# One program order for five engines and the DMA queue, written anew: x loads, context loads, stores and transposes in another sequence, and one scratch tile moved

## The chip, the cores and the metric

One core of a Trainium2 chip runs the whole program. The time is the device time of one execution in microseconds (us); the median of three runs is compared.

## What is computed

The reference is a gated layer over 2 x 1024 rows of width 2048, in float32:

```python
q1 = fake_quant(layernorm(x), x1_scale, x1_zp)      # 8-bit steps, kept as integers
q2 = fake_quant(ctx, x2_scale, x2_zp)               # (2, 2048, 2048)
x  = x + tanh(g_xattn[0]) * (q1 @ q2)
n  = layernorm(x)
logits = n @ route_w.T                              # 8 experts, the best one is taken
h  = n @ A[e].T                                     # rank 16 for each of the 8 experts
x  = x + tanh(g_ffn[0]) * (route_weight * h) @ Bw   # only the chosen expert counts
```

## The kernel before, in words

**Tiles.** The 2048 rows are 16 tiles t of 128 rows, tiles 0 to 7 of batch 0 and 8 to 15 of batch 1. For each tile TensorE computes four units (t, nb), 512 columns each, of 16 matmuls; `main(t, nb, run)` is a quarter of one, four matmuls. The context of a batch is quantised once into `q2`: 16 pieces of 1 MB per batch (`load_ctx(n)`, pieces 0 to 15 and 16 to 31). ScalarE quantises a piece from its landing place (`stage`, and early on `yT` and `y`) to int8 (`affine_ctx`), GpSimd or ScalarE casts it to bf16 (`widen_ctx`). A piece of batch 1 is cast when the main units of tile 7 for its column block are done.

**The way of a tile.** `load_x(t)`; VectorE's statistics (`stats1`); GpSimd's scale (`first_norm`); ScalarE to int8 (`affine_x`); GpSimd to bf16 (`widen_x`) in the single buffer q1. Then q1 is transposed: by TensorE for tiles 0 to 5 (`turn_q1`, read back by VectorE in `take_q1T`), by a DMA transpose for the others (`flip_q1`). Then the main units; VectorE adds each to x and takes statistics (`add_main`, `stats2_sum`); GpSimd's scale (`second_norm`); ScalarE writes the normed rows as a float16 high part and in full (`norm_high`, `norm_full`), GpSimd subtracts for the low part (`low_rows`). Both parts are transposed by DMA (`flip_high`, `flip_low`) for tiles 2 to 14, and by TensorE (`turn_y`) for 0, 1 and 15. TensorE multiplies them with the router and A (`h_rows_high`, `h_rows_low`, `h_group`), VectorE picks the expert (`gate`, about ten small instructions), TensorE turns the scaled result (`turn_wh`), ScalarE reads it (`take_wh`), TensorE makes four `expert_product(t, g)` of three matmuls each in two PSUM banks `outp`, VectorE adds each to x (`add_experts`), which frees the bank. `store(t)` writes the rows out.

**One tile is finished in another way.** `OUT_ACT = [14]`: for tile 14 ScalarE scales the product into a scratch tile (`scale_part`, line 835) and GpSimd adds it (`add_part`, line 612). The scratch tile lies in `yn`, the source of the flips.

**Places.** x tiles share eight homes (`HOME`, eight places for 16 tiles): `load_x(t)` waits until the tile that had the home before has been stored. x(8) takes the home of tile 3, x(9) that of tile 4, x(10) that of tile 5. `load_ctx(n)` from piece 18 on waits for `affine_ctx(n - 2)`.

**Order.** Nothing is scheduled by the machine: for each engine the calls stand in a list, one list for SP, GpSimd, ScalarE, VectorE and TensorE, and every call waits for its semaphores when its turn comes. All big transfers are issued from SP's list, lines 374 (x), 383 (ctx), 402 (stores), 413, 418 and 422 (flips). A call that waits holds up all that stand behind it on its engine. Engines are joined only by the semaphores.

## Time and profile before

| | us |
|---|---|
| median of 3 runs | 371.43 |
| lowest, highest | 370.81, 371.92 |
| the profiled execution | 371.31 |
| its span (first to last instruction) | 369.5 |
| TensorE busy (matmuls) | 335.8 |
| VectorE, ScalarE, GpSimd busy | 263.2, 193.9, 175.9 |

The span is the time of the profiled execution less 1.8 us around it. Busy time says how much an engine works, not whether it is waited for. In the timeline of an engine a bracket after a row gives the idle time before it and who ended that; the chain of waits follows the last instruction back to what released it, step by step. A DMA has two times: how long its issue held SP, and how long it took from issue to landing, which the chain shows.

### The profile page before, as it was taken

The page shows a single profiled execution, that of the slowest core. Times are in us where ns is not written, and L with a number is a line of the kernel's source. Part 1 is how long each engine was busy: PE and PEld are TensorE (multiplying, and loading weights), DVE is VectorE, ACT ScalarE, POOL GpSimd, SP SyncE. Part 2 cuts the span into 40 slices and gives each one's busy share as a digit, 9 for nine tenths or more (in the row PEclk, how much of TensorE's full clock was granted, in tenths as well). Part 3 has the DMA queues.
Part 4 walks back from the last instruction along what each step waited for, and adds up shares of the span by engine and source line. Part 5 has one row for each costly group of instructions (what it writes and reads, how often), then busy time and mean ns, then how long its engine had stood idle before and what let it go on. Part 6 is the DMA issues. An engine that isn't in the chain of part 4 may idle for free.

```text
span 369.5 us, 5800 instructions
## 1 busy us (share of the span) xinstructions
PE 335.8 (91%) x2214; PEld 183.7 (50%) x2214; DVE 263.2 (71%) x552; ACT 193.9 (52%) x124; POOL 175.9 (48%) x224
## 2 busy tenths in 40 slices
PE   0259999999999989999999889999999999999883
PEld 0124455555766644645464545564465546555361
DVE  3858895798968787783858769748748483774874
ACT  1698299766967480388996453424062424040060
POOL 2396575703334552385977238345257343423041
PEclk9999999999999999999999999999999999999999
DMA  7999998686679999999999799978659361974226
GB/s 313 390 353 395 396 347 307 244 306 260 231 243 227 198 368 194 356 255 289 163 331 259 196 355 157 291 132 269 114 229 172 129 129 30 184 235 96 114 116 227
DMA packets 98066, 88.68 MB, mean 240 GB/s; under 512 B 76004, under 2 KB 77028, under 8 KB 93924
## 3 DMA queue, kind: packets, MB, share of 16 engines
q1 hardware_dynamic: 98016, 88.15, 81.9%
q8 instruction: 26, 0.43, 0.5%
q14 instruction: 12, 0.10, 0.1%
q10 hardware_dynamic: 12, 0.00, 0.0%
HBM read 52.49 MB, written 16.78 MB: 187 GB/s over the span
## 4 chain that ended last, share of the span: by engine, by line
PE 64%; DMA 14%; DVE 9%; ACT 5%; SPq 3%; issue 3%; POOL 2%; ACTq 0%; DVEq 0%; POOLq 0%
PE main L1552 39%; PE outp L1552 5%; DMA xs<-in_x 4%; DVE bn L966 3%; PE hp L1580 3%; DMA qa<-q 3%; PE hp L1576 3%; PE hp L1577 3%; DMA stage<-in_ctx 3%; PE outp L1621 2%; PE outp L1623 2%; PE outp L1622 2%; ACT c L730 2%; ACT x L748 2%; DMA yT<-yn 2%
## 5 line engine op out<-in xcount | busy, mean ns | idle before, releaser
L1552 PE MATMUL main<-q,qa 128*128 128x512 bf16 x880 | 202.9, 384 | 4.5 <-DMA qa<-q 2.8
L1552 PEld LDWEIGHTS main<-q,qa 128*128 128x128 bf16 x880 | 85.5, 99 | 104.7 <-issue 5.3
L585 POOL TENSOR_TENSOR yn<-y,yn 128x2048 f16<-128x2048 f32 x13 | 53.0, 4079 | 31.8 <-ACT y L783 31.7
L1099 DVE SCALAR_TENSOR_TENSOR xs<-main,cc,xs 128x512 f32<-128x512 f32 x46 | 34.2, 743 | 32.2 <-PE main L1552 32.1
L730 ACT ACTIVATE c<-stage,zpc,inv 128x2048 int8<-128x2048 f32 x24 | 49.8, 2086 | 7.9 <-DMA stage<-in_ctx 7.9
L592 POOL CAST q<-c 128x2048 bf16<-128x2048 int8 x24 | 45.8, 1929 | 12.7 <-ACT c L730 10.1
L570 POOL TENSOR_SCALAR ve<-mv 128x1 f32<-128x1 f32 x16 | 3.5, 220 | 84.3 <-DVE mv L1106 84.3
L966 DVE BATCH_NORM_STATS2 bn<-xs 128x6 f32<-128x512 f32 x52 | 32.1, 680 | 14.4 <-DMA xs<-in_x 14.4
L777 ACT ACTIVATE yn<-xs,sc 128x2048 f16<-128x2048 f32 x11 | 23.0, 2093 | 35.6 <-POOL sc L579 35.6
L1153 DVE SCALAR_TENSOR_TENSOR xs<-outp,tsc,xs 128x512 f32<-128x512 f32 x48 | 33.9, 734 | 6.7 <-PE outp L1623 6.7
L748 ACT ACTIVATE x<-xs,sc 128x2048 int8<-128x2048 f32 x12 | 25.1, 2088 | 24.4 <-POOL sc L565 24.4
L1102 DVE BATCH_NORM_STATS2 bn<-xs 128x6 f32<-128x512 f32 x52 | 36.1, 694 | 1.8
L1576 PE MATMUL hp<-WT,yT 128*128 128x136 f16 x256 | 34.8, 223 | 0.9 <-DMA yT<-yn 0.7
L1577 PE MATMUL hp<-WT,yT 128*128 128x136 f16 x256 | 34.8, 223 | 0.0
L788 ACT ACTIVATE whT<-wp 128x256 f16<-128x256 f16 x16 | 6.0, 374 | 54.8 <-PE wp L1609 54.8
L600 POOL CAST q<-x 128x2048 bf16<-128x2048 int8 x12 | 22.7, 1892 | 11.8 <-ACT x L748 11.8
L1621 PE MATMUL outp<-BT,whT 128*128 128x512 f16 x64 | 24.3, 380 | 3.7 <-DVE xs L1153 3.0
L1576 PEld LDWEIGHTS hp<-WT,yT 128*128 128x128 f16 x256 | 25.0, 98 | 3.3 <-issue 2.0
L1577 PEld LDWEIGHTS hp<-WT,yT 128*128 128x128 f16 x256 | 25.0, 98 | 1.4
L1623 PE MATMUL outp<-BT,whT 128*128 128x512 f16 x64 | 24.3, 379 | 0.0
L1622 PE MATMUL outp<-BT,whT 128*128 128x512 f16 x64 | 24.3, 379 | 0.0
L1580 PE MATMUL hp<-WT,yT 128*128 128x136 f16 x256 | 23.2, 223 | 0.1
(131 smaller groups left out, 421.1 us busy)
## 6 DMA issues: line engine op xcount, KB each, us to landing
stage<-in_ctx SPq DMA_DIRECT2D x24, 1024.0 KB, 7.5
xs<-in_x SPq DMA_DIRECT2D x13, 1024.0 KB, 6.9
out<-xs SPq DMA_DIRECT2D x12, 1024.0 KB, 4.7
yT<-in_ctx SPq DMA_DIRECT2D x4, 1024.0 KB, 10.1
y<-in_ctx SPq DMA_DIRECT2D x4, 1024.0 KB, 11.2
c<-in_x SPq DMA_DIRECT2D x3, 1024.0 KB, 7.1
out<-c SPq DMA_DIRECT2D x3, 1024.0 KB, 4.3
c<-in_L_ffn_A SPq DMA_DIRECT2D x1, 1024.0 KB, 14.8
```

The lines of the kernel that those rows point to most:

```text
L585: pool.tensor_tensor(yn[:, 1, :], y[:, :], yn[:, 0, :], ALU.subtract).then_inc(s_ylo_made, 1)
L592: pool.tensor_copy(in_q2(piece), c8_of(piece)).then_inc(s_ctx_ready, 1)
L730: act.activation(c8_of(piece), place(piece), ACT.Identity, bias=zpc[:, 1:2], scale=inv[:, 1:2])\
L748: act.activation(x8[:, :], xcol(t, 0, D), ACT.Identity, bias=sc1[:, t, 2:3], scale=sc1[:, t, 1:2])\
L966: dve.bn_stats(bn1[:, t % 2, nb, :], xcol(t, nb * NW, (nb + 1) * NW)).then_inc(s_bn1_done, 1)
L1099: dve.scalar_tensor_tensor(out=xcol(t, c0, c1), in0=bank_of(n)[:, :], scalar=cc[:, :], in1=xcol(t, c0, c1), op0=ALU.mult, op1=ALU.add).the ...
L1102: dve.bn_stats(bn2[:, t % G, nb, :], xcol(t, c0, c1)).then_inc(s_bn2_done, 1)
L1153: dve.scalar_tensor_tensor(out=xcol(t, g * NW, (g + 1) * NW), in0=outp[g % 2][:, :], scalar=tsc[:, t:t + 1], in1=xcol(t, g * NW, (g + 1) * ...
L1552: last = pe.matmul(bank_of(n)[:, :], q1T(t)[:, k, :], q2[:, nb, k, :], start=(k == 0), stop=(k == KC - 1))
L1576: pe.matmul(hp[:, 0:WC], yT[:, 0, c, :], WT[:, c, 0:WC], start=(c == 0), stop=False)
L1577: pe.matmul(hp[:, 0:WC], yT[:, 0, c, :], WT[:, c, WC:2 * WC], start=False, stop=False)
L1580: return pe.matmul(hp[:, 0:WC], yT[:, 1, c, :], WT[:, c, 0:WC], start=False, stop=(c == KC - 1))
```

## The change

All five lists are written in another order. The calls are the same, in number and kind: 106 on SP, 85 on GpSimd, 122 on ScalarE, 251 on VectorE, 436 on TensorE. And the scratch tile of the scaled products of tile 14 moves from `yn` to the staging of the context, with the waits that follow from its place:

```diff
-        part = yn[:, :, :].rearrange("p a n -> p (a n)").bitcast(f32)
+        def part(t):
+            return stage[:, OUT_ACT.index(t) % 2, :]
...
             def scale_part(t, g):
                 n = NB * OUT_ACT.index(t) + g
-                if n < NB:
-                    act.wait_ge(s_yhiT_loaded, 16 * len(YN))
-                    act.wait_ge(s_yloT_loaded, 16 * len(YN))
-                else:
-                    act.wait_ge(s_part_added, n - NB + 1)
+                if n >= 2 * NB:
+                    act.wait_ge(s_part_added, n - 2 * NB + 1)
                 act.wait_ge(s_out_done, NB * t + g + 1)
                 act.wait_ge(s_tsc_done, t + 1)
-                act.activation(part[:, g * NW:(g + 1) * NW], outp[g % 2][:, :], ACT.Identity, bias=zero[:, :], scale=tsc[:, t:t + 1])\
+                act.activation(part(t)[:, g * NW:(g + 1) * NW], outp[g % 2][:, :], ACT.Identity, bias=zero[:, :], scale=tsc[:, t:t + 1])\
                    .then_inc(s_part_made, 1)
...
             load_ctx(0)
             load_ctx(1)
+            load_x(3)
             load_ctx(2)
...
-            load_x(3)
             load_x(4)
```

SP's list up to the flips: before, x(0) x(1) x(2), ctx(0) to (3), A, router, ctx(4) to (7), x(3) x(4), ctx(8) to (14), B, ctx(15) to (20), x(5), ctx(21) to (24). Now x(3) comes after ctx(1), ctx(15) before B, x(5) before ctx(20), and ctx(25) still ahead of the first flip. After the first flips (h, l and q for high, low and q1; s for store) the two lists are:

```
before: h2 l2 s0 h3 x6 l3 s1 c25 s2 | q6 h4 l4 x7 s3 c26 x8 c27 | q7 h5 l5 c28 c29 h6 l6 q8 | s4 c30 x9 c31 | h7 l7 s5 q9
        x10 x11 x12 | h8 l8 q10 s6 s7 | h9 l9 q11 x13 x14 | h10 l10 q12 s8 x15 | h11 l11 q13 s9 | h12 l12 q14 h13 l13 q15
        s10 s11 | h14 l14 s12 s13 s14 and the four quarters of 15
now:    h2 l2 s0 h3 x6 l3 s1 s2 | q6 h4 l4 x7 c26 c27 s3 c28 x8 c29 | q7 h5 l5 s4 h6 l6 q8 | x9 c30 c31 | h7 l7 s5 q9
        x10 x11 x12 | h8 l8 q10 h9 s6 | l9 q11 s7 x13 x14 | h10 l10 q12 h11 l11 q13 s8 s9 x15 | h12 l12 q14 h13 l13 q15
        h14 l14 | s10 s11 s12 s13 s14 and the four quarters of 15
```

SP, from the load of x(7) to the low flip of tile 5 (`xs<-in_x` is an x load, `out<-xs` a store, `stage<-in_ctx` a context piece, `qa<-q` the flip of q1, `yT<-yn` one of the normed rows). Before:

```order
35 L374 DMA xs<-in_x 128x2048
36 L402 DMA out<-xs 128x2048
37 L383 DMA stage<-in_ctx 128x4x512
38 L374 DMA xs<-in_x 128x2048
39 L383 DMA stage<-in_ctx 128x4x512
40 L413 DMA_TRANSPOSE qa<-q 128x16x128
41 L418 DMA_TRANSPOSE yT<-yn 128x16x128
42 L422 DMA_TRANSPOSE yT<-yn 128x16x128
43 L383 DMA stage<-in_ctx 128x4x512 x2
```

SP, the same place in the changed kernel (its lines are two higher):

```order
35 L376 DMA xs<-in_x 128x2048
36 L385 DMA stage<-in_ctx 128x4x512 x2
37 L404 DMA out<-xs 128x2048
38 L385 DMA stage<-in_ctx 128x4x512
39 L376 DMA xs<-in_x 128x2048
40 L385 DMA stage<-in_ctx 128x4x512
41 L415 DMA_TRANSPOSE qa<-q 128x16x128
42 L420 DMA_TRANSPOSE yT<-yn 128x16x128
43 L424 DMA_TRANSPOSE yT<-yn 128x16x128
44 L404 DMA out<-xs 128x2048
```

Two context pieces that came after the three flips now come before them, and two pieces stand ahead of store(3) instead of none.

ScalarE, from x(6) to x(8) (`c<-stage` quantises a context piece, `x<-xs` an x tile, `yn<-xs` is norm_high, `y<-xs` norm_full, `whT<-wp` take_wh). Before:

```order
51 L748 ACTIVATE x<-xs,sc 128x2048
52 L730 ACTIVATE c<-stage,zpc,inv 128x2048 x2
53 L788 ACTIVATE whT<-wp 128x256
54 L777 ACTIVATE yn<-xs,sc 128x2048
55 L748 ACTIVATE x<-xs,sc 128x2048
56 L783 ACTIVATE y<-xs,sc 128x2048
57 L788 ACTIVATE whT<-wp 128x256
58 L730 ACTIVATE c<-stage,zpc,inv 128x2048 x2
59 L748 ACTIVATE x<-xs,sc 128x2048
```

ScalarE, the same place in the changed kernel:

```order
50 L750 ACTIVATE x<-xs,sc 128x2048
51 L732 ACTIVATE c<-stage,zpc,inv 128x2048
52 L790 ACTIVATE whT<-wp 128x256
53 L732 ACTIVATE c<-stage,zpc,inv 128x2048 x3
54 L779 ACTIVATE yn<-xs,sc 128x2048
55 L790 ACTIVATE whT<-wp 128x256
56 L750 ACTIVATE x<-xs,sc 128x2048
57 L785 ACTIVATE y<-xs,sc 128x2048
58 L750 ACTIVATE x<-xs,sc 128x2048
```

ctx(26) and ctx(27), which stood behind norm_high(5), affine_x(7) and take_wh(4), now stand ahead of all three.

TensorE, in tile 5, from `main(5,1,1)` on (`L1552 main` counts matmuls, `L1609 wp` is turn_wh(3), the triples on outp are the products of tile 3). Before:

```order
316 L1552 MATMUL main<-q,qa 128x512 x16
317 L1609 MATMUL wp<-idh,whs 128x128 x2
318 L1552 MATMUL main<-q,qa 128x512 x4
319 L1621 MATMUL outp<-BT,whT 128x512
320 L1622 MATMUL outp<-BT,whT 128x512
321 L1623 MATMUL outp<-BT,whT 128x512
```

TensorE, the same place in the changed kernel:

```order
313 L1550 MATMUL main<-q,qa 128x512 x24
314 L1607 MATMUL wp<-idh,whs 128x128 x2
315 L1550 MATMUL main<-q,qa 128x512 x32
316 L1619 MATMUL outp<-BT,whT 128x512
317 L1620 MATMUL outp<-BT,whT 128x512
318 L1621 MATMUL outp<-BT,whT 128x512
```

The first product of tile 3 moves behind all main units of tile 5; h_rows_high(4) then stands between its second and third. VectorE's list moves add_experts(3, g) behind add_main(5,3) in the same way.

## Rows read from the trace of the kernel before

**Rows 1.** The page, part 1: busy us (share of the span) x instructions.

```profile
PE 335.8 (91%) x2214; PEld 183.7 (50%) x2214; DVE 263.2 (71%) x552; ACT 193.9 (52%) x124; POOL 175.9 (48%) x224
```

**Rows 2.** TensorE's timeline (start, us), rows with idle time; one stretch (length, busy).

```profile
27.97 1.03 PE L1480 MATMUL turn<-idb,q 128*128 128x128 bf16 x8 [1.03 <-DVE q L1002]
...
131.36 0.39 PE L1621 MATMUL outp<-BT,whT 128*128 128x512 f16 x1 [1.58 <-DVE xs L1153]
...
167.09 1.25 PE L1552 MATMUL main<-q,qa 128*128 128x512 bf16 x5 [1.08 <-DMA qa<-q]
...
213.50 7.08 PE L1552 MATMUL main<-q,qa 128*128 128x512 bf16 x32 [1.74 <-DMA qa<-q]
...
335.40 0.22 PE L1576 MATMUL hp<-WT,yT 128*128 128x136 f16 x1 [0.72 <-DMA yT<-yn]
...
180.00:210.00 30.00, 29.63 (x210) 16.22 (x208) 20.87 (x50) 23.70 (x14) 21.17 (x19) 1.00 0.97 246
```

**Rows 3.** The chain of waits, 117 to 139 us: start, us, what.

```profile
117.85 3.07 SPq L418
...
120.96 6.95 DMA xs<-in_x
...
127.94 2.48 DVE bn L966 x4
...
134.64 3.45 PE main L1552 x16
```

**Rows 4.** The chain of waits, 144 to 167 us.

```profile
144.11 7.61 DMA xs<-in_x
...
151.74 2.48 DVE bn L966 x4
...
158.40 1.90 POOL q L600
160.36 6.69 DMA qa<-q
```

**Rows 5.** The chain of waits, 185 to 214 us.

```profile
185.57 5.30 DMA out<-xs
...
191.27 9.46 DMA stage<-in_ctx
...
208.88 4.57 DMA qa<-q
```

**Rows 6.** Stretches: length, busy of PE, PEld, DVE, ACT, POOL, clock, DMA share, GB/s.

```profile
140.00:150.00 10.00, 10.00 (x68) 5.40 (x66) 6.55 (x10) 0.00 (x0) 0.54 (x1) 1.00 1.11 209
150.00:160.00 10.00, 10.00 (x66) 5.21 (x64) 8.22 (x23) 5.86 (x3) 4.48 (x11) 1.00 0.99 377
160.00:170.00 10.00, 8.91 (x42) 3.93 (x41) 6.52 (x12) 7.20 (x6) 7.72 (x13) 1.00 1.18 215
```

**Rows 7.** SP's timeline: issue start, how long the issue held SP.

```profile
145.53 0.43 SPq L402 DMA_DIRECT2D out<-xs  x1
...
169.13 1.15 SPq L383 DMA_DIRECT2D stage<-in_ctx  x2
...
191.81 8.75 SPq L418 DMA_TRANSPOSE yT<-yn  x1
```

**Rows 8.** ScalarE's timeline, 150 to 166 us.

```profile
152.25 2.09 ACT L777 ACTIVATE yn<-xs,sc 128x2048 f16<-128x2048 f32 x1 [13.48 <-POOL sc L579]
156.24 2.09 ACT L748 ACTIVATE x<-xs,sc 128x2048 int8<-128x2048 f32 x1 [1.89 <-POOL sc L565]
...
160.22 0.36 ACT L788 ACTIVATE whT<-wp 128x256 f16<-128x256 f16 x1
...
163.57 2.09 ACT L730 ACTIVATE c<-stage,zpc,inv 128x2048 int8<-128x2048 f32 x1 [1.01 <-DMA stage<-in_ctx]
```

**Rows 9.** VectorE's timeline, 18 to 28 us: the casts of x(1) and x(2).

```profile
18.68 1.16 DVE L1002 CAST q<-x 128x2048 bf16<-128x2048 int8 x1
...
24.96 2.95 DVE L1002 CAST q<-x 128x2048 bf16<-128x2048 int8 x1 [3.30 <-ACT x L748]
```

**Rows 10.** The chain of waits at 341 us, and ScalarE's timeline at 354 us.

```profile
341.24 0.95 PE hp L1580 x16
...
353.75 0.78 ACT L835 ACTIVATE yn<-outp,zero,tsc 128x512 f32<-128x512 f32 x1
```

More of the change, by code:

```diff
@@ L496, in _ @@
             flip_q1(10)
+            flip_high(9)
             store(6)
-            store(7)
-            flip_high(9)
             flip_low(9)
             flip_q1(11)
+            store(7)
             load_x(13)
@@ L511, in _ @@
             flip_q1(13)
+            store(8)
             store(9)
+            load_x(15)
             flip_high(12)
@@ L518, in _ @@
             flip_q1(15)
+            flip_high(14)
+            flip_low(14)
             store(10)
             store(11)
-            flip_high(14)
-            flip_low(14)
             store(12)
@@ L631, in _ @@
             widen_ctx(11)
+            widen_x(4)
             widen_ctx(12)
@@ L884, in _ @@
             affine_x(5)
+            take_wh(1)
             norm_high(3)
-            take_wh(1)
             norm_full(3)
-            affine_ctx(23)
             take_wh(2)
@@ L908, in _ @@
             widen_ctx(23)
+            take_wh(5)
             affine_ctx(28)
+            affine_ctx(29)
             widen_ctx(26)
-            take_wh(5)
-            affine_ctx(29)
-            widen_ctx(27)
             norm_high(7)
             norm_full(7)
+            widen_ctx(27)
+            affine_x(9)
             affine_ctx(30)
+            affine_ctx(31)
             widen_ctx(30)
-            affine_ctx(31)
             widen_ctx(31)
-            affine_x(9)
             take_wh(6)
@@ L1289, in _ @@
             add_main(4, 0)
+            add_main(4, 1)
             gate(1)
@@ L1314, in _ @@
             add_main(5, 1)
+            add_main(5, 2)
+            add_main(5, 3)
+            stats2_sum(5)
             add_experts(3, 0)
@@ L1318, in _ @@
             add_experts(3, 3)
-            add_main(5, 2)
-            add_main(5, 3)
-            stats2_sum(5)
+            gate(4)
             stats1(7)
-            gate(4)
             tile_terms(6)
             add_main(6, 0)
+            add_experts(4, 0)
             add_main(6, 1)
             stats1(8)
+            add_experts(4, 1)
             add_main(6, 2)
@@ L1387, in _ @@
             stats1(14)
-            add_main(11, 2)
             add_main(11, 3)
-            add_experts(8, 3)
             stats2_sum(11)
             tile_terms(12)
+            add_experts(8, 3)
+            add_experts(9, 0)
             add_main(12, 0)
             add_main(12, 1)
-            gate(10)
-            stats1(15)
-            add_main(12, 2)
-            add_experts(9, 0)
             add_experts(9, 1)
             add_experts(9, 2)
-            add_experts(9, 3)
+            gate(10)
+            add_main(12, 2)
             add_main(12, 3)
@@ L1404, in _ @@
             tile_terms(13)
+            add_experts(9, 3)
             add_main(13, 0)
             add_main(13, 1)
+            stats1(15)
             gate(11)
             add_experts(10, 0)
-            add_main(13, 2)
             add_experts(10, 1)
             add_experts(10, 2)
+            add_main(13, 2)
             add_main(13, 3)
@@ L1421, in _ @@
             add_experts(11, 1)
+            add_main(14, 0)
+            add_main(14, 1)
+            add_experts(11, 2)
+            add_main(14, 2)
             add_main(14, 3)
             stats2_sum(14)
-            add_experts(11, 2)
             add_experts(11, 3)
+            add_experts(12, 0)
             gate(13)
@@ L1762, in _ @@
             h_rows_low(2)
+            main(4, 2, 3)
+            expert_product(1, 0)
             main(4, 3, 0)
@@ L1910, in _ @@
             main(10, 2, 1)
+            expert_product(7, 2)
             main(10, 3, 0)
@@ L1913, in _ @@
             main(10, 2, 2)
+            main(10, 2, 3)
             main(10, 3, 2)
-            main(10, 2, 3)
+            main(10, 3, 3)
+            expert_product(7, 3)
             turn_wh(8)
-            main(10, 3, 3)
             h_rows_high(9)
-            h_rows_low(9)
             expert_product(8, 0)
@@ L1944, in _ @@
             main(12, 0, 0)
+            main(12, 1, 0)
+            main(12, 1, 1)
             main(12, 0, 1)
             main(12, 0, 2)
-            main(12, 1, 0)
-            h_rows_high(10)
+            main(12, 1, 2)
             main(12, 0, 3)
-            main(12, 1, 1)
-            main(12, 1, 2)
             main(12, 1, 3)
-            h_rows_low(10)
+            expert_product(9, 1)
+            expert_product(9, 2)
             main(12, 2, 0)
-            main(12, 3, 0)
-            main(12, 3, 1)
             main(12, 2, 1)
```

439 lines of the change are left out of this document (215 added, 224 removed).

## The prediction

> **What bounds the kernel now.** I read the page's engine row first: TensorE is busy for 335.8 of 369.5 us, so at most 33.7 us of its idle time can be removed, whatever is reordered [rows 1]. Next I read TensorE's own timeline for the rows with an idle time in brackets [rows 2]. From 27.97 us to the last norm there are only four with more than half a microsecond: 1.58 before 131.36, 1.08 before 167.09, 1.74 before 213.50 and 0.72 before 335.40. A stretch of 30 us from 180 shows 29.63 busy, so about 0.4 us more is lost in small pieces there [rows 2]. Together that is 5.5 us. Everything else between 28 and 347 us is work which the change doesn't shorten: no instruction is added or taken away. So the change can win little more than 5.5 us in the middle; it can lose any amount.
>
> Then I asked what ended each of the four waits, in the chain of waits. All go back to the one DMA queue.
> - 131.36: TensorE waits for an outp bank. VectorE frees it behind the statistics of x tile 6, whose load left at 120.96 and took 6.95 us, right after a flip whose issue held the queue for 3.07 us [rows 3].
> - 167.09: the flip of q1(7) took 6.69 us from 160.36, and it could leave only when GpSimd's cast of x(7) ended, which goes back to the load of x(7): 7.61 us from 144.11, then its statistics at 151.74 [rows 4].
> - 213.50: the flip of q1(9) left at 208.88. ScalarE quantises x(9) late because ctx(31) took 9.46 us to land (200.73), behind store(4) with 5.30 us, ctx(30) and x(9) [rows 5].
> - 335.40: the high flip of tile 14 is late; store(10) and store(11) stand ahead of it in SP's order.
>
> **How a flip and a load share the queue.** Three windows show it: 209 GB/s in 140 to 150 us (flips and a load), 377 in 150 to 160 (loads and one store), 215 in 160 to 170 (flips and loads) [rows 6]. A 1 MB load in a full queue costs 1.05 MB / 377 GB/s = 2.8 us. A flip that meets an empty queue lands after 4.57 us (208.88, [rows 5]). The issue of the flip at 191.81 held SP for 8.75 us, until 200.56, when ctx(31) landed (200.73) [rows 5, 7]: a flip goes behind all loads ahead of it, and SP stands still for that time. The same at 160.36: ctx(27) landed by 163.57 (ScalarE's wait for it ends there, [rows 8]), the flip at 160.36 + 6.69 = 167.05, that is 3.5 us after the last load. The Trainium skill, page "DMA: Bandwidth & Descriptors", section "Issuing engines are not separate DMA queues", says that DMAs from all issuers run on the same 16 engines and interleave. If that were all, a flip wouldn't wait for earlier loads, the flip in term 3 below would land about 0.9 us earlier, and the sum would be 0.9 us lower; the 8.75 us row speaks against it.
>
> **The change, part by part.** I keep one account: how far TensorE is behind (+) or ahead (-) of the kernel before at equal work. Four matmuls of a quarter unit take 3.45 / 4 = 0.86 us [rows 3], an expert product (three of the same size) 0.65.
>
> 1. *Start: +0.2 (-0.5 to +1.0).* x(3) goes ahead of ctx(2) and ctx(3), which so land 2.8 us later, and both halves of q1(2) are turned before main(0,0,1). Ahead of that TensorE now waits for widen_x(2) on VectorE. That copy took 2.95 us from 24.96 while GpSimd cast ctx pieces [rows 9], and its like, widen_x(1), 1.16 [rows 9]. It would start near 23.6, wait out GpSimd's cast and end near 26.1; two reads of turn banks follow. TensorE restarts near 26.8 instead of 27.97 [rows 2], but has one more turn behind it and no main(0,0,1). It reaches the end of main(0,0,3) within half a microsecond of before. The later flow of pieces 4 to 7 has about 1.5 us to spare. The bounds: the earlier restart kept whole, or one more cast waited for.
>
> 2. *Up to tile 5: -0.5 (0 to -1.6).* ctx(25) no longer stands between the stores after flip_low(3), and h_rows_high(2) stands one quarter unit (0.86 us) earlier, which lets flip_high(3) and so x(6) leave up to 0.86 us earlier than 117.85 and 120.96 [rows 3]. The bank wait at 131.36 shrinks by that, less some 0.4 us (my estimate: part of one main addition) for gate(1), which now stands behind add_main(4,1). The account after it: -0.3.
>
> 3. *Tiles 5 to 7: +1.6 (0 to +2.8).* This is where the change costs. The products of tile 3 now come after all of tile 5's main units. Of those, six quarter units (5.2 us) and the 32 high matmuls of tile 4 (16 of that size take 0.95, [rows 10], so 1.9 us) lie ahead of expert_product(3,3) that lay behind it. store(3), which left at 145.53 [rows 7], can't leave before about 150.5. x(8) needs the place that store(3) empties, so x(8) and ctx(29) leave after it has landed. In numbers: x(7) lands near 151, ctx(26) and ctx(27), now right behind it, near 154 and 156.5, store(3) near 159, x(8) near 164, ctx(29) near 167, and the flip of q1(7) 3.5 us later: 170.3. A second chain says nearly the same. ScalarE takes ctx(26) and ctx(27) (2.1 each) ahead of norm_high(5), take_wh(4) and affine_x(7), which started at 152.25, 160.22 and 156.24 [rows 8]. Now: 156.5 + 2.1 = 158.6, norm_high 160.7, take_wh 161.0, affine_x(7) 163.0, cast 1.9 [rows 4] 164.9, flip 4.6: 169.5. TensorE asks for q1(7) at 167.09 - 1.08 = 166.0 in the kernel before [rows 2] and would now, with three more products done (1.95) and 0.3 ahead, at 167.7. It waits 2.6 us where it waited 1.1. Equal work stood at 167.09 + 1.95 = 169.0 before. The account: +1.3 at main(7,0,0). On the way expert_product(4,0) waits for take_wh(4), which is inside the same wait and costs nothing more.
>
> 4. *Tiles 7 to 9: -2.1 (-2.7 to -0.5).* ctx(28) and ctx(29) left at 169.13 behind the flips before [rows 7]; now they have landed ahead of them. Between q1(7) and the high flip of tile 7 stand seven transfers where nine stood. Two loads are 5.6 us, of which the later start (3.2 us) takes back more than half. ctx(31) lands near 197 instead of 200.73, affine_x(9) no longer stands behind affine_ctx(30) and (31), widen_x(9) ends near 206, and the flip of q1(9) lands near 210.4. TensorE comes for it near 210.7. So the 1.74 and the 0.4 go. The account: -0.8.
>
> 5. *Tile 14: -0.7 (-0.7 to 0).* The last flips now come before store(10) and store(11), and h_rows_high(14) later in TensorE's order. The 0.72 us wait goes.
>
> 6. *The staging: 0.* scale_part(14,0) no longer waits for the last flips, and writes stage instead of yn. The low flip of 14 was read by TensorE at 341.24, the scaling began at 353.75, after the product [rows 10]. The wait had been over for 12 us. The wait on the part before last is never taken, with one tile in OUT_ACT.
>
> 7. *Tail and all else: +0.3 (0 to +2.5).* In the last 20 us product (14,1) and turn_y(15,3) swap places with h groups; by the rows' lengths gate(15) starts 0.2 later at most. Of 1,000 calls that moved, a few will meet a wait that I don't see; before, TensorE was full from 214 to 335 us, so there it can't win, only lose.
>
> Sum: 0.2 - 0.5 + 1.6 - 2.1 - 0.7 + 0 + 0.3 = -1.2. The profiled execution took 371.3 us (span 369.5), the median of the three is 371.4; 371.4 - 1.2 = 370.2, rounded to 370.1 for the restart, whose gain I took at the low side.
>
> **The rivals.**
> - *The queue is in time for q1(7).* If store(3)'s late start doesn't hold x(8) and ctx(29) until 167, for instance because ctx(26) and (27) move at full rate in the now unbroken run of loads, the 2.6 us wait disappears and terms 4 and 5 stay. 370.1 - 2.6 = 367.5. For it: 377 GB/s in the one window of loads alone. Against it: ScalarE's chain gives 169.5 without store(3).
> - *Nothing is gained at 213.* The later flips of tile 5 carry their delay on: the queue was full from 140 to 215 us, and a load saved early is waited for later. Term 4 falls to zero and term 3 is part of one account with it: about 371.5 to 372.
> - *Slower: x(8) stops VectorE.* stats1(8) stands ahead of add_experts(4,1), which frees the bank for expert_product(4,3). If x(8) lands after 167 instead of 164 (store(3) 2 us later and a flip caught between), statistics (2.5, as at 151.74 in [rows 4]) and one add hold TensorE from 168.5 on, q1(7) lands near 173, and with ScalarE late again for tile 8's flip the gain at 213 goes too: +3, 373.2 to 374. It decides from x(8) at 167.
> - *The order does nothing measurable*: gains and losses of one microsecond cancel, 371 to 372. That can't be told from the second rival by time alone.
>
> **How the numbers follow.** Forecast (369.2 to 371.2): 0.40, of which a bit over half lies below 370.3. In time for q1(7), 366.5 to 369.2: 0.22. Nothing gained or cancelled, 371.2 to 372.5: 0.18. Slower: 0.20. The range that leaves out no more than two in ten reaches from 367.0 to 373.2. A measurement of this kernel tells 0.3% (1.1 us) from no change. Faster by more: 0.22 + 0.26 = 0.48; within: 0.14 + 0.18 = 0.32, less 0.01 for the edges; slower: 0.20 and that edge, 0.21.
>
> **What would show it.** In the new profile: a wait of TensorE of 2 to 4 us for a flip near 170, with ScalarE's norm of tile 5 near 159 (term 3); no wait of TensorE near 213 and ctx(31) landed before 198 (term 4); none at 335 (term 5); the bank wait at 131 still there, about 0.8 (term 2). Wrong would be: no wait near 170 (the first rival), a wait above 4 us there with VectorE idle for x(8) (the third), or several new waits between 215 and 335.

## The result, and the profile after

The changed kernel is slower. In nine runs each it took 373.88 us in the median (372.26 to 375.95), the kernel before 371.43 (369.52 to 372.02): ratio 1.0075, 95% interval 1.0052 to 1.0099. The prediction was 370.1 us, range 367.0 to 373.2. So it has the sign wrong, and the time lies outside its range. Of all executions of this study three lay far outside the rest, one each in the runs from_8_x9_three (606.64 us), ctx25_ahead (910.74) and x9_alone (2003.06): they are in the medians below and not in the ratios.

The profiled execution is the lowest of the nine, 372.26 us (span 370.4), and that matters below. Its engine row answers to [rows 1]: the work is the same.

```profile
PE 334.9 (90%) x2214; PEld 183.8 (50%) x2214; DVE 262.7 (71%) x552; ACT 193.4 (52%) x124; POOL 176.9 (48%) x224
```

TensorE's timeline after the change, the rows with idle time that answer to [rows 2] (start, length, in brackets the idle time before and its releaser):

```profile
90.00 1.09 PE L1570 MATMUL turn<-idf,y 128*128 128x128 f32 x8 [1.24 <-ACT y L759]
...
131.83 0.39 PE L1619 MATMUL outp<-BT,whT 128*128 128x512 f16 x1 [1.01 <-DVE xs L1151]
...
171.10 1.25 PE L1550 MATMUL main<-q,qa 128*128 128x512 bf16 x5 [1.92 <-DMA qa<-q]
...
212.93 2.33 PE L1550 MATMUL main<-q,qa 128*128 128x512 bf16 x10 [0.93 <-DMA qa<-q]
...
329.28 1.90 PE L1550 MATMUL main<-q,qa 128*128 128x512 bf16 x8 [0.29 <-DMA qa<-q]
```

The wait near 131 has shrunk from 1.58 to 1.01, that for q1(9) from 1.74 to 0.93, that at 335 is gone. The wait for q1(7) grew from 1.08 to 1.92. New is 1.24 us at 90.00, in the norm of tile 0, where the prediction had no term, and 0.38 at 167.50, for the bank of `expert_product(4,3)`. At equal work TensorE is 0.9 us behind in this execution.

Why is the norm of tile 0 late? Two things hold it back. The first is GpSimd's. Its timeline in `second_norm(0)`, changed kernel, and VectorE's beside it:

```profile
85.58 2.24 POOL L581 TENSOR_TENSOR sc<-mv,sc 128x1 f32<-128x1 f32 x1
```

```profile
85.41 2.35 DVE L1182 SCALAR_TENSOR_TENSOR BT<-c,bmax,BT 128x2048 f16<-128x2048 f32 x1 [0.77 <-ACT BT L812]
```

The last instruction of the five works on one element per partition and took 2.24 us; it ended with VectorE's `low_b()`, which the new list puts ahead of `add_main(1,3)`. In the kernel before the same instruction took 0.19, when `low_b()` came later:

```profile
85.72 0.19 POOL L579 TENSOR_TENSOR sc<-mv,sc 128x1 f32<-128x1 f32 x1
```

The second is ScalarE's. The new list has the context piece `affine_ctx(19)` ahead of `norm_rows(0)` (L759), which started at 85.94 before:

```profile
85.28 2.08 ACT L732 ACTIVATE c<-stage,zpc,inv 128x2048 int8<-128x2048 f32 x1
87.85 2.09 ACT L759 ACTIVATE y<-xs,sc 128x2048 f32<-128x2048 f32 x1 [0.48 <-POOL sc L581]
```

ScalarE was busy with the piece until about 87.4, so GpSimd's late end at 87.82 held it for the last 0.48 us only. Each of the two is enough for most of the delay. The profile of a later run, late_x_slack, has the same lists in this stretch and shows the second alone. There `low_b()` started at 86.29, `second_norm(0)` had ended at 85.6 after 1.75 us, and the wait of TensorE was the longest of all, 1.66 us at 90.28. ScalarE in it:

```profile
86.16 2.08 ACT L732 ACTIVATE c<-stage,zpc,inv 128x2048 int8<-128x2048 f32 x1
88.15 2.08 ACT L759 ACTIVATE y<-xs,sc 128x2048 f32<-128x2048 f32 x1
```

### The profile page after: what moved, and what is told of

It is laid out like the page before. It is cut to its first block, busy times and chain, and to the rows that moved or that the text cites. A ratio compares the mean times of both kernels' runs of the same rounds, so it can differ in the third digit from the quotient of the medians.

```text
span 370.4 us, 5798 instructions
## 1 busy us (share of the span) xinstructions
PE 334.9 (90%) x2214; PEld 183.8 (50%) x2214; DVE 262.7 (71%) x552; ACT 193.4 (52%) x124; POOL 176.9 (48%) x224
## 4 chain that ended last, share of the span: by engine, by line
PE 39%; DMA 19%; DVE 15%; ACT 10%; POOL 8%; issue 6%; SPq 2%; ACTq 0%; DVEq 0%; POOLq 0%
PE main L1550 26%; ACT c L732 6%; DMA stage<-in_ctx 6%; DMA xs<-in_x 5%; DVE bn L964 5%; DMA qa<-q 5%; POOL yn L587 3%; PE hp L1578 2%; PE outp L1619 2%; PE hp L1574 2%; PE hp L1575 2%; DVE xs L1151 2%; PE outp L1621 2%; PE outp L1620 2%; DMA prow<-in_g_ffn 2%
## 5 line engine op out<-in xcount | busy, mean ns | idle before, releaser
L594 POOL CAST q<-c 128x2048 bf16<-128x2048 int8 x24 | 45.0, 1896 | 9.0 <-ACT c L732 8.6
```

Of the source, the lines that this page charges most:

```text
L594: pool.tensor_copy(in_q2(piece), c8_of(piece)).then_inc(s_ctx_ready, 1)
```

## The parts of the change, one at a time

Runs with the same time in the third column ran beside one another and share the runs of the kernel before, to which the ratio is. Most medians are of 10 to 12 executions; from_tile_8 has four, norm0_first, from_8_x9_later and ctx25_ahead have six.

| run | us | before | ratio, 95% interval |
|---|---|---|---|
| again | 374.15 | 371.06 | 1.0070 (1.0043 to 1.0098) |
| tiles_0_to_4 | 373.10 | 371.06 | 1.0069 (1.0043 to 1.0094) |
| tiles_5_to_7 | 371.66 | 371.06 | 1.0020 (0.9990 to 1.0050) |
| from_tile_8 | 376.27 | 371.06 | 1.0130 (1.0095 to 1.0165) |
| start_alone | 372.11 | 371.10 | 1.0021 (0.9987 to 1.0054) |
| tiles_1_to_4 | 373.14 | 371.10 | 1.0061 (1.0031 to 1.0092) |
| late_x_slack | 373.26 | 371.10 | 1.0067 (1.0037 to 1.0098) |
| norm0_first | 375.88 | 371.10 | 1.0139 (1.0100 to 1.0179) |
| low_b_early | 371.82 | 371.17 | 1.0011 (0.9988 to 1.0035) |
| ctx19_early | 371.42 | 371.17 | 0.9999 (0.9980 to 1.0019) |
| ctx25_ahead | 375.54 | 370.87 | 1.0126 (1.0087 to 1.0165) |
| from_8_x9_later | 377.70 | 371.17 | 1.0189 (1.0160 to 1.0218) |
| from_8_x9_three | 372.90 | 370.87 | 1.0058 (1.0030 to 1.0087) |
| whole_but_8_9 | 373.00 | 370.87 | 1.0071 (1.0042 to 1.0099) |
| last_part | 370.89 | 371.17 | 0.9973 (0.9953 to 0.9993) |
| last_part_and_x9 | 368.79 | 370.87 | 0.9942 (0.9921 to 0.9964) |
| x9_alone | 368.66 | 371.27 | 0.9942 (0.9915 to 0.9968) |
| bank_wait_too | 368.79 | 371.27 | 0.9924 (0.9897 to 0.9951) |

**The change again.** No edit.

> The changed kernel once more, on the chip on which the three halves of the change run beside it. Its nine runs went from 372.3 to 376.0 us with a median 2.45 us above the kernel before, but the profiled one was the lowest, and in it TensorE is only 0.9 us behind at the end. Theory 1 (the waits seen in the profile are the whole cost, the rest is scatter): the difference to the kernel before comes out at +0.9 to +1.5 us, and a new profile shows the same waits: 1.4 at turn_y(0,0) near 90, 2.1 at main(7,0,0) near 171, 1.1 near 213, 0.5 near 329. Theory 2 (the order is fragile: a wait grows from run to run that the lowest run doesn't show): the difference stays at +2.0 to +3.0 us, and a new profile of a slower execution shows one or two waits more, or the same ones 1 to 2 us longer.

The difference stays at 3.1 us by the medians (2.6 by the ratio), and the profile, of 375.91 us this time, has waits that the lowest execution doesn't show. TensorE:

```profile
170.10 0.39 PE L1619 MATMUL outp<-BT,whT 128*128 128x512 f16 x1 [2.50 <-DVE xs L1151]
...
201.12 1.90 PE L1550 MATMUL main<-q,qa 128*128 128x512 bf16 x8 [1.15 <-DVE xs L1097]
```

and VectorE, which holds it up, waits for two x loads:

```profile
166.67 2.47 DVE L964 BATCH_NORM_STATS2 bn<-xs 128x6 f32<-128x512 f32 x4 [2.50 <-DMA xs<-in_x]
...
194.77 2.47 DVE L964 BATCH_NORM_STATS2 bn<-xs 128x6 f32<-128x512 f32 x4 [3.39 <-DMA xs<-in_x]
```

In the lowest execution the same two rows began at 164.07 and 192.40. The first is the mechanism of the prediction's third rival: x(8) lands 2.6 us later, `stats1(8)` stands ahead of `add_experts(4,1)`, and the bank for `expert_product(4,3)` comes late. Theory 2 holds: the lowest execution is not the usual one. Of the 3.7 us between the two executions' spans, 2.5 had come by the last products (365.85 against 363.35). The other 1.2 came behind them, where TensorE's granted clock was 0.66 in 365 to 370 us, against 0.90 in the lowest.

**Three parts.** The edit: each of the five lists is the old one, but for one stretch that is the new one.

> The kernel before with the new order only up to the middle of tile 5 (on SP up to load_x(7)); behind that the old one. Theory 1: the new wait at turn_y(0,0) near 90 costs 1.0, the start gives 0.2, the wait for the bank near 131 shrinks by some 0.4; of the 0.5 us that remain the wait for q1(7) near 167 takes part or all, since x(7) lands as early as before: -0.3 to +0.5 us against the kernel before. Theory 2 (the early part is what makes the whole slow): +1.5 us or more.

> The kernel before with the new order only from the middle of tile 5 to the end of tile 7 (on SP from store(3) to the flip of q1(8)): the products of tile 3 behind all main units of tile 5, ctx(26) and ctx(27) ahead of store(3), ctx(28) and ctx(29) ahead of the flips. Theory 1: the flip of q1(7) lands near 171, TensorE is 2.1 us behind at main(7,0,0), and the wait of 1.74 at main(9,0,0) goes since ctx(31) and the flip of q1(9) come earlier: +0.3 to +1.0 us at the end. Rival (the queue stays full, nothing is given back at 213): +2 to +3 us at the end, with the wait at 213 still above 1 us.

> The kernel before up to the end of tile 7 and the new order behind it (with the scratch tile in the staging). Theory 1: the wait of 0.72 near 335 goes, one of 0.46 for the flip of q1(15) near 329 comes, the rest is as before: -0.5 to +0.5 us. Theory 2 (what the lowest run doesn't show lies here, late in the program, where TensorE was full before): +1.0 to +2.0 us.

2.0, 0.6 and 5.2 us are 7.8, where the whole costs 3.1. The parts don't add up. Tiles 5 to 7 behave as theory 1 said (the interval takes in no change). In their profile, which is the highest of its twelve executions, TensorE is 1.4 us behind at 168.96 and some 3.4 at 200 (an estimate from the matmuls left to do), and 1.8 behind main(9,0,0): a part is given back there. The early part costs 2.0 us, as its theory 2 said, and more than its visible wait of 0.97 at 89.74. The part from tile 8 is the surprise. TensorE's row in it:

```profile
200.53 3.32 PE L1552 MATMUL main<-q,qa 128*128 128x512 bf16 x8 [4.23 <-DVE xs L1099]
```

VectorE ahead of it:

```profile
187.46 0.27 DVE L1106 BATCH_NORM_AGGREGATE mv<-bn 128x2 f32<-128x24 f32 x1
194.20 2.47 DVE L966 BATCH_NORM_STATS2 bn<-xs 128x6 f32<-128x512 f32 x4 [6.48 <-DMA xs<-in_x]
...
199.72 0.75 DVE L1099 SCALAR_TENSOR_TENSOR xs<-main,cc,xs 128x512 f32<-128x512 f32 x1
```

`gate(6)` stands ahead of `add_main(8,0)` in both lists; the new one has `stats1(9)` ahead of both. VectorE stands idle for 6.48 us for x(9), and the add that frees TensorE's bank starts at 199.72; in the kernel before it started at 193.83. In the whole change TensorE reaches that place 2 us later, because tile 7 has already cost it that, and x(9) lands 1.8 us earlier (192.40): the wait is 0.04 there. One delay covers another, in this execution; in that of 375.91 us the wait was 1.15.

## Which call it is

**x(8) and x(9) on VectorE, in the whole change.**

```diff
-            stats1(8)
             add_experts(4, 1)
             add_main(6, 2)
+            stats1(8)
...
-            stats1(9)
             gate(6)
+            stats1(9)
```

> The changed kernel with two calls moved on VectorE alone: stats1(8) stands behind add_main(6,2) instead of ahead of add_experts(4,1), stats1(9) behind gate(6) instead of ahead of it. In the lowest run of the changed kernel x(8) landed at 164.05 and x(9) at 192.37 and TensorE waited 0.55 and 0.04 us behind them; in the profile of 375.9 us they landed at 166.65 and 194.75, stats1 held VectorE, and TensorE waited 2.66 us for the outp bank at expert_product(4,3) and 1.31 us at main(8,2,0). Theory S (the new order gives a late x load straight on to TensorE, that is what the usual run pays and the lowest doesn't): both waits are gone in the profile or below 0.3 us, and the median comes 1 to 2 us below that of the changed kernel (374.15), near 372.5. Rival C (the spread is that of the clock near the end and of the loads, TensorE only waits at the next place, main(7,0,0) and main(9,0,0)): waits of 2 us or more at main(7,0,0) and of 1 us or more at main(9,0,0) take their place, the median moves by less than 0.5 us.

Rival C is nearer. Both waits are gone, and in their place stand 1.76 us at main(7,0,0), 171.64, and 1.87 at main(9,0,0), 214.36. The median is 0.9 us below that of the run again, the ratio 0.0003 below: a gain isn't shown, and one of 1 us isn't excluded.

**x(9) on VectorE alone, from tile 8 on.** The edit: `stats1(9)` behind `add_main(8, 1)`.

> The kernel of the run from_tile_8 (old order up to tile 7, new order behind it, 376.27 us, 5.2 above the kernel before) with one call of VectorE moved: stats1(9) behind add_main(8,1) instead of ahead of gate(6) and add_main(8,0). In its profile x(9) landed at 194.17, stats1(9) and gate(6) held add_main(8,0) until 199.72, TensorE waited 4.40 us at main(8,2,0), and the granted clock was at half for 3.4 us behind that wait. Theory S (a load's landing stands in VectorE's order ahead of the add that frees TensorE's bank, and that is the whole 5.2): the wait at main(8,2,0) and the half-speed stretch go, the median falls to 370.5 to 372.0 us. Rival C (the supply bounds, the wait only moves to main(9,0,0), since the flip of q1(9) lands no earlier): a wait of 3 us or more at main(9,0,0), median above 373.5 us.

Theory S falls in this form: 377.7 us, in six executions. The 4.23 us are gone and three waits stand in their place:

```profile
200.09 0.39 PE L1621 MATMUL outp<-BT,whT 128*128 128x512 f16 x1 [1.97 <-DVE xs L1153]
...
207.15 1.02 PE L1552 MATMUL main<-q,qa 128*128 128x512 bf16 x4 [2.71 <-POOL q L592]
...
209.54 2.00 PE L1580 MATMUL hp<-WT,yT 128*128 128x136 f16 x16 [1.37 <-DMA yT<-yn]
```

But rival C's place, main(9,0,0), isn't it. GpSimd's timeline names the cause of the last two: it stands idle for 7.90 us for the statistics of x(9), and `low_rows(7)` and the casts wait behind.

```profile
199.53 0.21 POOL L555 TENSOR_SCALAR ve<-mv 128x1 f32<-128x1 f32 x1 [7.90 <-DVE mv L968]
...
201.09 4.08 POOL L585 TENSOR_TENSOR yn<-y,yn 128x2048 f16<-128x2048 f32 x1
205.11 3.73 POOL L592 CAST q<-c 128x2048 bf16<-128x2048 int8 x2
```

**x(9) on three engines.** The edit: `stats1(9)` as in the last run, and

```diff
 # GpSimd
-            first_norm(9)
             low_rows(7)
             widen_ctx(28)
             widen_ctx(29)
+            first_norm(9)
 # ScalarE
-            affine_x(9)
             affine_ctx(30)
             affine_ctx(31)
+            affine_x(9)
```

> The kernel of the run from_tile_8 (376.27 us) with x(9) moved back on three engines: stats1(9) on VectorE behind add_main(8,1), first_norm(9) on GpSimd behind widen_ctx(29), affine_x(9) on ScalarE behind affine_ctx(31). With VectorE's call alone moved the wait of 4.40 us at main(8,2,0) was gone but the median was 377.7: TensorE waited 2.13, 2.87 (for GpSimd's casts, which stood behind first_norm(9)) and 1.53 us (for the low flip of tile 7, whose low_rows(7) stood behind it too). Theory S (x(9) stands ahead of tile 7's and the context's work on three engines, and that is the price): none of the four waits above 1 us between 190 and 212, no half-speed stretch there, median 370.8 to 372.5 us. Rival C (the order of TensorE from tile 8 on asks for more than the queue gives, whoever stands first): the waits return elsewhere before 216, median above 374 us.

Theory S nearly, with all three: 376.3 and 377.7 us become 372.9, where it had 370.8 to 372.5 and rival C above 374. GpSimd's `low_rows(7)` starts at 192.06, the casts at 196.08. Three calls account for 3.4 of the 5.2 us by the medians, for 2.7 by the ratios. In its profile, the lowest of its executions, 1.96 us at 199.99 is left, for `add_experts(5,1)` behind `stats1(9)`, and 0.39 at 210.43; the rest of the part I didn't take apart.

**The whole without tiles 8 and 9.** The edit: the old lists in that stretch of the changed kernel.

> The changed kernel with the old order only in tiles 8 and 9 (on SP from ctx(30) to the flip of q1(10), on TensorE from expert_product(5,0) to main(9,1,3)); there x(9) stands behind the work of tile 7 on all engines again. Theory S: the wait of 0.04 to 1.31 us at main(8,2,0) goes, TensorE is no more than 1 us later at main(9,0,0), and the median falls by 0.5 to 1.5 us against the changed kernel's 374.15, to 372.7 to 373.6. Rival (in the whole the delay of tiles 5 to 7 covers x(9), and the old order of tile 8 brings the wait of 1.7 at main(9,0,0) back): no change or slower, 374 to 375 us.

The ratio is 1.0071, that of the whole (1.0070), which speaks for the rival. The median, 373.00, lies where theory S had it, but the kernel before was at 370.87 beside it and at 371.06 beside the run again. With intervals of 0.3% to either side a share of 1 us isn't excluded, 5.2 us are. So the 3 us of the change are not the 5.2 us of this part: in the whole the delay ahead of tile 8 covers most of it.

## The norm of tile 0, and the early part

> The kernel before with the new order only in the first part (on SP up to ctx(15) and B, on TensorE up to main(0,2,2), some 55 us): x(3) ahead of ctx(2), the turns of q1(2) and the reads of them in another order. The new order up to the middle of tile 5 cost 2.0 us in the median and 0.2 us in its profile. Theory C (the start): in one execution of the kernel before's order the granted clock rose at 26.4 us and TensorE was 1.5 us ahead, in two others at 32.7; with the new start, whose wait of 2.06 ends at 26.87, it rose at 31.1 to 31.8 in three: so +0.5 to +1.0 us in the median and no execution below 370. Theory N (the early loss is all at the norm of tile 0): -0.3 to +0.3 us.

> The kernel before with the new order only between main(0,2,2), some 55 us, and the middle of tile 5 (on SP from ctx(15) to load_x(7)). It holds low_b() ahead of add_main(1,3), affine_ctx(19) ahead of norm_rows(0), and ctx(25) ahead of the first flips. Theory N: the wait near 90 is there with 1.1 to 1.4 us, the bank wait near 131 shrinks by 0.4, and the median is +1.0 to +1.7 us, so that this part is most of the 2.0 us that the new order up to tile 5 costs. Theory C (most of it is the start): below +0.7 us.

1.0 us, not beyond its uncertainty, and 2.0 us: most of the early part lies in tiles 1 to 4, more than theory N's 1.0 to 1.7. In its profile the wait at turn_y(0,0) is there with 0.96, and TensorE is 1.8 us behind at main(7,0,0).

The start stays open. Two executions of start_alone were below 370 us, against theory C. But the profiles show something that favours it. Eight turns take 0.61 us at full clock (35.93 in the kernel before), sixteen 1.06 (39.36 in the changed one). In six of the thirteen profiles with the old start the eight turns near 28 us took 0.62, and TensorE was an estimated 0.6 to 1.0 us ahead at 60 us; in the other seven, the kernel before's among them, they took 1.03. In all seven with the new start the sixteen turns near 27 us took 1.86 or 1.87. So the new start may forgo a gain that the old one has in some executions; no run tests it.

**Both causes taken away, in the whole change.** The edit: `low_b()` behind `add_main(1, 3)`; `affine_ctx(19)` behind `norm_rows(0)`, and `(20)` behind `high_part(0, 1)`.

> The changed kernel with the norm of tile 0 cleared: low_b() on VectorE stands behind take_q1T(4,0), take_q1T(4,1) and add_main(1,3) again, so that it no longer runs beside second_norm(0) on GpSimd, and affine_ctx(19) and affine_ctx(20) stand behind norm_rows(0) on ScalarE. Theory: second_norm(0) takes 1.75 us again instead of 3.8, norm_rows(0) starts near 86 instead of 87.85, the wait of 1.1 to 1.4 us at turn_y(0,0) near 90 is gone, and the median falls by 0.7 to 1.0 us against the changed kernel (374.15), to 373.2. Rival (the 1 us is absorbed later, where TensorE waits for the queue at 167 to 171 and 213 anyway): the wait is gone, the waits near 171 and 213 grow by as much, the median moves by less than 0.4 us. If second_norm(0) still takes above 3 us, the stretched instruction wasn't due to low_b.

`second_norm(0)` took 1.75 us again and the wait at 90 was gone, but the median rose to 375.88: my edit set a wait of its own. ScalarE took the pieces later, stood 2.09 us for piece 21, and `high_part(0,2)` stood behind that piece:

```profile
96.74 2.09 ACT L732 ACTIVATE c<-stage,zpc,inv 128x2048 int8<-128x2048 f32 x1 [2.09 <-DMA stage<-in_ctx]
98.74 1.06 ACT L766 ACTIVATE yT<-turn 128x512 f16<-128x512 f32 x2
```

TensorE waited 2.04 us there, and its granted clock was 0.66 in 100 to 105 us. It is the same pattern as x(9): a call that waits for a load stands ahead of a tile's small steps.

**One call each, in the kernel before.** The edits: `low_b()` behind `take_scales()`; `affine_ctx(19)` ahead of `norm_rows(0)`.

> The kernel before with one call of VectorE moved as in the new order: low_b() directly behind take_scales(), ahead of take_q1T(4,1) and add_main(1,3). Theory: in all profiles in which low_b ran inside second_norm(0) that took 3.5 to 3.8 us on GpSimd, in all others 1.75. So it takes 3.5 or more here, norm_rows(0) starts 1.8 us later, TensorE waits about 1 us at turn_y(0,0) near 89, and since flips and loads follow TensorE's work nothing takes that back: +0.7 to +1.3 us in the median. Rival (the old order of ScalarE, without affine_ctx(19) ahead, and the waits for q1(7) and q1(9) take it up): the median moves by less than 0.4 us.

> The kernel before with one call of ScalarE moved as in the new order: affine_ctx(19) ahead of norm_rows(0). Theory: ctx(19) has landed by 85, so norm_rows(0) starts at 87.5 to 88.2 instead of 85.94, a wait of 1.0 to 1.5 us at turn_y(0,0) comes though second_norm(0) takes 1.75 us as before, and the median rises by 0.7 to 1.3 us; the two causes cover one another, which is why the run that took both away only moved the wait. Rival (absorbed later): less than 0.4 us.

The first has the mechanism: `second_norm(0)` took 3.66 us, and the instruction that was stretched is another of the five,

```profile
84.86 2.16 POOL L576 TENSOR_SCALAR sc<-rs 128x1 f32<-128x1 f32 x1
```

and TensorE waited 0.82 at 89.75. The median rose by 0.65 us, which the interval doesn't tell from none. The second is a miss: the piece had landed and was taken at 83.83, `norm_rows(0)` started at 85.83, no wait came, and the time didn't move. In the profiles of the changed kernel's order that start varies with the landing of the pieces ahead, from 83.73 (again) to 86.16 (late_x_slack), so this run doesn't clear the call there.

**Piece 25 ahead of the first flips.** The edit: `load_ctx(25)` behind `load_ctx(24)` on SP, and `affine_ctx(21)` to `(23)` earlier on ScalarE, without which it can't be loaded.

> The kernel before with ctx(25) ahead of the first flips on SP, as in the new order, and what that needs on ScalarE: affine_ctx(21), (22) and (23) each one or two calls earlier, behind norm_rows(1), norm_high(2) and high_part(1,1). The part tiles_1_to_4 cost 2.0 us in the median; low_b() early alone cost 0.65 us and affine_ctx(19) early alone 0.25, neither beyond the uncertainty. Theory (the third change of that part is the rest): the high flip of tile 2 leaves 1 us or more later than at 108.85, x(6) follows, and the median rises by 0.7 to 1.3 us. Rival (as the prediction's step 2 had it: ctx(25) out of the stores' way helps): the wait near 131 shrinks, the median stays or falls by up to 0.5 us, and the 2.0 us come only from the causes together.

1.26% slower, far more than expected, but by a wait of its own: 2.75 us at 105.47, turn_y(1,2), behind ScalarE's piece again. The granted clock behind it was 0.66 in 105 to 110. The high flip of tile 2 left at 112.92 instead of 108.85, x(6) at 124.97 instead of 120.96. This profile is the lowest of its executions, 372.42 us, and ends 1.1 us behind that of the kernel before: most of the 1.26% isn't in it. It shows which way the calls of this stretch push, not what they cost in the change, where the order of TensorE beside them is another. How the 2.0 us of tiles 1 to 4 divide stays open.

## What beats both

The 5.2 us had a reverse side. In the kernel before ScalarE's `affine_x(9)` stood behind `affine_ctx(31)` and `widen_ctx(31)`:

```profile
200.75 2.09 ACT L730 ACTIVATE c<-stage,zpc,inv 128x2048 int8<-128x2048 f32 x1 [1.95 <-DMA stage<-in_ctx]
202.94 1.91 ACT L736 ACTIVATE q<-c 128x2048 bf16<-128x2048 int8 x1
204.75 2.08 ACT L748 ACTIVATE x<-xs,sc 128x2048 int8<-128x2048 f32 x1
```

x(9)'s scale was ready before 201.8, and the flip that TensorE waits for 1.74 us hangs on it [rows 2]. The cast of piece 31 isn't asked for before main(8,3,3) at 209.3.

**The last part, then with x(9), then x(9) alone.** The edit of the last: on ScalarE, in the kernel before,

```diff
             affine_ctx(31)
-            widen_ctx(31)
             affine_x(9)
+            widen_ctx(31)
```

> The kernel before with the new order only in the last part (on SP behind flip_low(11), on TensorE from the end of tile 13's main units), the scratch tile still in yn: the flips of tile 14 ahead of store(10) and store(11), h_rows_high(14) one quarter unit later, and the new order of the tail. Theory (the prediction's step 5): the wait of 0.72 to 0.93 near 335 goes, no other comes, the median falls by 0.5 to 0.9 us. Rival: in the profiles with the new order a wait of 0.46 stands at main(15,0,0) for the flip of q1(15), and the end of the program was 0.6 to 0.8 us further behind than main(9,1,0): then the median rises by 0.2 to 0.7 us.

> A version meant to beat both: the kernel of the run last_part (370.89 us, 0.27% below the kernel before) with one call more moved, affine_x(9) on ScalarE between affine_ctx(31) and widen_ctx(31) instead of behind both. In its profile affine_x(9) started at 204.01, though first_norm(9) had ended at 200.90, widen_x(9) waited 5.26 us for it and TensorE 1.68 us at main(9,0,0) for the flip. Theory: affine_x(9) starts near 202.1, widen_x(9) 1.9 us earlier, the flip of q1(9) lands near 211, the wait at main(9,0,0) falls below 0.3 us, widen_ctx(31) ends near 206 while main(8,3,3) asks for it at 208.6; median 369.3 to 370.0 us. Rival (the flip leaves behind store(5), which landed at 206.7, or the work behind tile 9 waits by as much): the wait stays above 1 us or comes back before 260, the median falls by less than 0.4 us.

> The kernel before with one call of ScalarE moved: affine_x(9) between affine_ctx(31) and widen_ctx(31) instead of behind both. Together with the last part it gave 0.58% (368.79 against 370.87 us), the last part alone 0.27%. Theory (the two are independent, each behind its own wait): the wait of 1.74 us at main(9,0,0) goes, the one of 0.7 to 0.9 near 335 stays, and the median falls by 0.9 to 1.5 us. Rival (only together, since the clock near the end or the flips of tile 14 depend on the first gain): below 0.4 us.

The last part alone is 0.27% faster, as step 5 said: in it the wait near 335 is gone, and no other stands at main(15,0,0). The one call of ScalarE is worth 0.58%, 2.2 us (1.2 to 3.2), more than the theory's 0.9 to 1.5. In its profile TensorE is 1.2 us ahead of the kernel before when it starts tile 7, most of it since the first 60 us, and 3.6 us ahead once it is past main(9,0,0) (estimates from the matmuls left to do). The call so gives some 2.4 us here: the wait of 1.74 and smaller ones ahead of it. From 165.86 to 331.98, where the wait for tile 14's flip stands with 0.60 as expected, there is none of 0.3 us, and ScalarE reads

```profile
199.22 2.09 ACT L730 ACTIVATE c<-stage,zpc,inv 128x2048 int8<-128x2048 f32 x1 [1.96 <-DMA stage<-in_ctx]
201.22 2.08 ACT L748 ACTIVATE x<-xs,sc 128x2048 int8<-128x2048 f32 x1
203.21 1.89 ACT L736 ACTIVATE q<-c 128x2048 bf16<-128x2048 int8 x1
```

The two gains together (368.79 us, below the theory's 369.3 to 370.0) can't be told from this one alone: both ratios are 0.9942.

**A wait further ahead.** The edit: on top of both, `add_experts(2, 0)` ahead of `stats1(6)`.

> The kernel of the run last_part_and_x9 (368.79 us) with one call of VectorE moved: add_experts(2,0) ahead of stats1(6), behind take_q1T(5,0), so that the bank for expert_product(2,2) is free before the load of x(6) lands. Theory (waits of TensorE add up): the wait of 1.35 us near 130 goes, main(5,0,2) waits 0.3 to 0.6 us for take_q1T(5,1) instead, and the median falls by 0.5 to 0.8 us. Rival (the flip of q1(7), whose chain goes back to the load of x(7) and not to TensorE, takes it): the wait at main(7,0,0) near 165 grows from 0.9 to about 1.5 us, the median moves by less than 0.3 us.

The median is unchanged at 368.79. The ratio is 0.9924 where it was 0.9942, and the intervals overlap: the runs tell neither the theory's 0.5 to 0.8 us nor the rival's nothing. In the profile the bank wait is gone, and three places take it, in order:

```profile
131.43 1.04 PE L1552 MATMUL main<-q,qa 128*128 128x512 bf16 x4 [0.69 <-DVE qa L1016]
138.94 0.39 PE L1621 MATMUL outp<-BT,whT 128*128 128x512 f16 x1 [0.45 <-ACT whT L788]
...
167.88 2.33 PE L1552 MATMUL main<-q,qa 128*128 128x512 bf16 x10 [1.22 <-DMA qa<-q]
```

In this execution what was won ahead of the flip of q1(7) was waited for there: 1.22 us, where last_part_and_x9 had 0.73.

## Why the prediction was wrong

1. *Start, +0.2:* not contradicted, and not confirmed (1.0021, interval 0.9987 to 1.0054, that is -0.5 to +2.0 us).
2. *Up to tile 5, -0.5:* **the step that failed first.** The bank wait did shrink, by 0.57. But the step looked for changes only where the kernel before had a wait. The new 1.24 us at turn_y(0,0) stood at a place where TensorE had been full, and tiles 1 to 4 alone cost 2.0 us, not a gain. It was ScalarE's piece and GpSimd's stretched instruction, of which the step has neither. Term 7 named such waits and gave them +0.3.
3. *Tiles 5 to 7, +1.6:* the timetable held nearly to the microsecond. `affine_ctx(26)` started at 153.33 and (27) at 156.28, store(3) left at 151.81, x(8) landed at 164.05, the flip of q1(7) at 171.05 (predicted: 154, 156.5, 150.5, 164, 170.3). It was made for an execution in which nothing is late. x(8) at 164.05 already cost 0.38 us, so the third rival decides from 164 and not from 167, as I had put it; in the next profile VectorE had x(8) at 166.67, and TensorE lost 2.5 us. I had the mechanism, and took its chance as that of one timetable against another, not of one execution against another. That the median, 373.88, lies in this rival's 373.2 to 374 is luck: with its wait taken away in late_x_slack the ratio stayed. For the rest the step was sound: TensorE waited 1.92 us for q1(7), not 2.6, and went from 0.5 to 2.1 us behind, the +1.6 of the term.
4. *Tiles 7 to 9, -2.1:* **wrong.** I read "affine_x(9) no longer stands behind affine_ctx(30) and (31)" as a gain alone. It means as well that these stand behind x(9), with `low_rows(7)` on GpSimd and `add_main(8,0)` on VectorE. The wait at main(9,0,0) fell by 0.8 in the lowest execution, and TensorE went from being 2.75 us late in front of it to 0.86 late after it, where the account had it 0.8 ahead; but the part by itself is 5.2 us slower. The change of ScalarE's order that does bring the gain, without the other, is a single call.
5. *Tile 14, -0.7:* right; the last part alone gave 0.28 us in the median and 0.27% in the ratio, 1.0 us (interval 0.3 to 1.7). In the whole 0.29 us came back at main(15,0,0).
6. *The staging, 0:* not measured by itself; nothing in the profiles speaks against it.
7. *The sum.* The parts alone are 7.8 us and the whole 3.1. Adding signed terms assumes that each wait is paid in full, and that TensorE's lateness leaves the loads alone. Neither is so: a delay of TensorE moves the flips (108.85 became 110.27 in the profile of tiles_1_to_4), so the loads behind them, so the next wait. A term for the clock was missing too: a wait can cost more than itself (last section).

So the first step to fail is term 2: tiles 1 to 4, forecast at -0.5 us, cost 2.0 by themselves, and with the start the ratio is 1.0069, as much as the whole (1.0070). The part is shown, and in it the wait at turn_y(0,0) with its two causes; what makes up the rest of the 2.0 us stays open.

The profile of one execution hid half of it. Over all runs of this study the lowest and highest of the changed kernel are 371.6 and 376.3. The kernel before varies too: term 7 took TensorE as full from 214 to 335 us, but three profiles with the old order there (ctx19_early, low_b_early, last_part) have a wait of 1.20, 0.87 and 0.79 us near 258.

The clock isn't the cause of the difference. Of the 135 executions of the kernel before that ran beside these runs, the 56 with a mean granted clock of 0.997 or more have a median of 370.5 us, the others 371.55; of the changed kernel's 20 the eleven have 373.8, the others 374.7. It is slower by about 3 us in either group.

## To carry to other kernels

In a list that is worked through in order, put a call that waits for a load behind the calls that free something the bound engine needs, on each engine that the loaded tile passes; look for such inversions in all lists before adding up waits. Three such calls were worth 2.7 to 3.4 us here, and two others, in late_x_slack, nothing that could be told. When reckoning with one profiled execution, shift each load by the 2 to 3 us by which x(8) and x(9) moved between two executions of one kernel, and see which waits appear. And a wait removed ahead of one that has another cause may be waited for there.

## What the runs showed of the hardware

- **A small GpSimd instruction can last as long as a large one of VectorE.** With `low_b()` (two inputs in SBUF, 2.35 us) running inside `second_norm(0)`, its five small instructions took 3.5 to 3.8 us in six profiles, in the fourteen others 1.75. The Trainium skill, page "SBUF — State Buffer", section "SBUF: two separate sides", says that VectorE and GpSimd share a port pair as an exclusive lock, held for the whole instruction by the one that starts first, and that a VectorE operation with two SBUF inputs takes it against a GpSimd operation that reads SBUF. By that rule the stretched instruction must end with VectorE's; the trace agrees: 85.58 + 2.24 = 87.82 against 85.41 + 2.35 = 87.76.
- **TensorE's granted clock fell to half behind some of its longer waits.** Behind the 4.23 us in the run from_tile_8 (stretch, length, busy of five engines, clock, DMA share, GB/s):

```profile
195.00:200.00 5.00, 1.30 (x7) 0.39 (x4) 4.69 (x17) 1.75 (x2) 2.78 (x6) 1.00 1.07 359
200.00:205.00 5.00, 4.47 (x15) 1.71 (x16) 3.62 (x6) 5.00 (x4) 5.00 (x3) 0.66 0.50 104
```

  that is 1.2 instead of 2.4 GHz for about two thirds of the second stretch. The eight matmuls behind the wait took 3.32 us, where eight take 1.90 at full clock: 1.4 us on top of the wait. The same shows behind 2.04 us in norm0_first, 2.75 in ctx25_ahead (0.66 in the five us behind each), 2.33 in tiles_5_to_7 (0.68 in 170 to 175), and 2.71 and 1.37 in from_8_x9_later (0.72 in 210 to 215). After the 2.50 us in the run again it stayed full. The price of a wait is not the wait alone, and not the same each time.
